# Both first layer norms of a two-block graph kernel from the statistics of x, with x loaded from two queues

## The reference, cut to what matters

```python
def _layernorm(x, axis=-1, eps=1e-05):
    m = jnp.mean(x, axis=axis, keepdims=True)
    v = jnp.var(x, axis=axis, keepdims=True)
    return (x - m) / jnp.sqrt(v + eps)

xn = _layernorm(x, axis=-1)                  # read by the graph branch and by the mix branch
x = x + _L0_gnn_ref(xn, ...) + _L0_mix_ref(xn[None], ...)[0]

# first lines of _L0_mix_ref
xn = _ln(x, g1, be1)                         # a second layer norm, of the first one's output, with scale and bias
kqv = xn @ Wkqv + bkqv
k, q, v = jnp.split(kqv, 3, axis=-1)
```

## Time and profile before

| | us |
|---|---|
| median of three runs | 1988.69 |
| span of the profiled execution, first to last instruction | 1983.8 |
| PE busy in it | 1641.4 |
| DVE busy | 798.2 |
| ACT busy | 506.5 |
| POOL busy | 391.0 |

### The profile page before, as it was taken

How to read it: one execution, slowest core, us unless ns; L and a number is a source line. 1 busy time by engine, 2 the same in 40 slices (tenths; PEclk the granted TensorE clock), 3 DMA queues, 4 the chain that set the end, 5 groups by cost and what they waited for, 6 DMA issues and landing times.

```text
span 1983.8 us, 19802 instructions
## 1 busy us (share of the span) xinstructions
PE 1641.4 (83%) x7770; PEld 1121.7 (57%) x7770; DVE 798.2 (40%) x1511; ACT 506.5 (26%) x734; POOL 391.0 (20%) x248
## 2 busy tenths in 40 slices
PE   1999979989998849888888887899888751999895
PEld 1547645456555638677777763465765641656452
DVE  5021051399502652477777863360334224111100
ACT  1101102012301032477777751100214110101000
POOL 3100021020201120244444423200211002222112
PEclk9999999989998969899999998999998855999997
DMA  4000010100020010101000003000200452699993
GB/s 169 0 0 1 0 44 0 58 1 1 41 86 0 6 64 33 46 14 27 14 13 14 22 8 142 5 22 0 85 0 1 177 224 98 266 406 402 404 418 129
DMA packets 23236, 170.74 MB, mean 86 GB/s; under 512 B 4259, under 2 KB 4805, under 8 KB 16886
## 3 DMA queue, kind: packets, MB, share of 16 engines
q1 hardware_dynamic: 19568, 164.44, 21.0%
q0 software_dynamic: 3584, 5.12, 1.2%
HBM read 153.06 MB, written 16.49 MB: 85 GB/s over the span
## 4 chain that ended last, share of the span: by engine, by line
PE 58%; DMA 15%; DVE 13%; ACT 6%; issue 4%; POOL 2%; another core or an unknown queue 1%; SPq 0%; DVEq 0%; POOLq 0%; ACTq 0%
PE psum L839 15%; DMA out_x<-arena,idx 12%; PE psum L849 9%; PE psum L866 6%; PE psum L980 6%; PE psum L1065 4%; PE psum L858 4%; PE psum L1053 3%; DVE arena_r L1449 3%; PE psum L1035 2%; DMA xf_dram<-arena 2%; DVE neg_max L1428 2%; ACT arena_r L762 1%; DVE ln_st L1219 1%; DVE arena L1227 1%
## 5 line engine op out<-in xcount | busy, mean ns | idle before, releaser
L839 PE MATMUL psum<-arena 125*128 125x512 f32 (+3 forms) x864 | 306.5, 516 | 14.4 <-DMA arena<-in_w_in 11.6
L839 PEld LDWEIGHTS psum<-arena 125*128 125x128 f32 (+1 forms) x864 | 164.1, 190 | 156.2 <-issue 142.2
L866 PE MATMUL psum<-arena 128*125 128x512 f32 (+3 forms) x464 | 162.6, 509 | 17.1 <-DVE arena L1556 9.0
L541 POOL TENSOR_SCALAR arena<-arena,row_inv 125x1250 f32<-125x1250 f32 x40 | 138.4, 3459 | 192.3 <-DVE row_inv L1436 192.3
L1200 PE MATMUL psum<-arena 128*39 128x512 f32 (+1 forms) x704 | 159.1, 609 | 13.2 <-DMA arena<-in_w_down 10.2
L1053 PE MATMUL psum<-ident,arena 125*125 125x125 f32 x800 | 125.6, 283 | 49.8 <-DVE arena_r L1449 48.5
L1449 DVE TENSOR_TENSOR arena_r<-psum,arena_r 125x500 fp32r<-125x500 f32 x200 | 131.9, 672 | 42.1 <-ACT arena_r L762 32.3
L1053 PEld LDWEIGHTS psum<-ident,arena 125*125 125x125 f32 x800 | 102.9, 188 | 63.0 <-DVE arena_r L1449 58.3
L762 ACT ACTIVATE arena_r<-psum 125x500 fp32r<-125x500 f32 x200 | 114.3, 586 | 88.0 <-PE psum L1053 87.8
L866 PEld LDWEIGHTS psum<-arena 128*125 128x125 f32 (+2 forms) x464 | 81.2, 191 | 95.2 <-issue 71.4
L980 PE MATMUL psum<-arena 125*125 125x512 bf16 (+1 forms) x588 | 119.8, 359 | 12.8 <-DVE arena L1340 11.3
(11 more groups left out here) (279 smaller groups left out, 2051.4 us busy)
## 6 DMA issues: line engine op xcount, KB each, us to landing
arena<-in_w_down SPq DMA_DIRECT2D x32, 2816.0 KB, 23.5
arena<-in_w_up SPq DMA_DIRECT2D x32, 682.5 KB, 19.4
a_spill<-arena SPq DMA_DIRECT2D x1, 6103.5 KB
arena<-a_spill SPq DMA_DIRECT2D x1, 6103.5 KB
bc<-k_dram SPq DMA_DIRECT2D x16, 312.5 KB, 4.2
gw<-in_gw SPq DMA_DIRECT2D x2, 2048.0 KB, 10.6
arena<-in_wkqv SPq DMA_DIRECT2D x1, 3072.0 KB, 16.4
arena<-in_x SPq DMA_DIRECT2D x10, 250.0 KB
```

Source lines behind the costliest of these rows:

```text
L541: pool.tensor_scalar(PR[i], PR[i], row_inv[:, i:i + 1], None, ALU.mult).then_inc(p_even, 1)
L839: ins = pe.matmul(o[0:w, lo:hi], lhs(c, m), rhs(c)[:, lo:hi], start=c == 0, stop=c == k - 1)
L866: ins = pe.matmul(o[0:p, 0:w], lhs(c, t), rhs(c, t), start=c == 0, stop=c == k - 1)
```

## The change

The order of the norms is turned round. The statistics are taken once, of x. For a row with variance v, the first norm's output has mean 0 and variance v / (v + e), so the second norm of it is (x - m) / sqrt(v (1 + e) + e * e). GpSimd makes that root for each group, and then the first norm's own root for all ten tiles in one pair of instructions (`xn_rs`, semaphore `xn_rstd`). VectorE writes `XH1` straight from X, a group behind the statistics, and writes `XN` after it. SyncE issues the even tiles of x and `wkqv` right behind them. ScalarE's queue issues the odd tiles and `vec`. GpSimd's bias addition now waits for both norms.

```diff
-LN_ORDER = [(n, g) for n in ("xn", "mix1", "mix2") for g in range(3)]
+LN_ORDER = [(n, g) for n in ("mix1", "mix2") for g in range(3)]
...
-            for t in range(TILES):
+            for t in range(0, TILES, 2):
                 load(f"x{t}", X[:, t], x_v[:, t])
-            load("vec", vec[:], a["vec"])
+            load("wkqv", WKQV, a["wkqv"].rearrange("p (k n) -> p k n", k=C))
             load("edge_rows", edge_rows_i, a["dst_rows"])
             load("edges", edge_i[:, 0:EDGE_TILES], a["src_cols"])
             load("edges", edge_i[:, EDGE_TILES:2 * EDGE_TILES], a["dst_cols"])
-            load("wkqv", WKQV, a["wkqv"].rearrange("p (k n) -> p k n", k=C))
...
-            for g in range(3):
-                rstd("xn", g)
+            for g, (lo, hi) in enumerate(GROUPS):
+                pool.wait_ge(ln_mv, LN_TILES["mix1", g])
+                pool.tensor_scalar(ln_rs[:, lo:hi], ln_mv_t[:, lo:hi, 1], 1.0 + LN_EPS, LN_EPS * LN_EPS,
+                                   ALU.mult, ALU.add).then_inc(ln_eps, 1)
+                pool.wait_ge(ln_eps, LN_NUMBER["mix1", g] + 1)
+                pool.tensor_tensor(ln_rs[:, lo:hi], ln_rs[:, lo:hi], minus_half[:, lo:hi], ALU.pow).then_inc(ln_rstd, 1)
+            done(pool.tensor_scalar(xn_rs[:], ln_mv_t[:, :, 1], LN_EPS, None, ALU.add))
+            pool.tensor_tensor(xn_rs[:], xn_rs[:], minus_half[:], ALU.pow).then_inc(xn_rstd, 1)
...
-            for g in range(3):
-                rstd("mix1", g)
-
             pool.wait_ge(loads["b2"], 16)
-            pool.wait_ge(ln_out, TILES)
+            pool.wait_ge(ln_out, 2 * TILES)
...
+            x_v = a["x"].rearrange("(t p) d -> p t d", p=TOK)
+            for t in range(1, TILES, 2):
+                act.dma_start(X[:, t], x_v[:, t]).then_inc(loads[f"x{t}"], 16)
+            act.dma_start(vec[:], a["vec"]).then_inc(loads["vec"], 16)
             act.wait_ge(loads["vec"], 16)
...
             for g in range(3):
-                stats("xn", g, X, lambda t: dve.wait_ge(loads[f"x{t}"], 16))
-            for g in range(3):
-                normalise("xn", g, X, XN)
-
-            for g in range(3):
-                stats("mix1", g, XN, lambda t: dve.wait_ge(ln_out, LN_OUT["xn"] + t + 1))
-            for g in range(3):
-                normalise("mix1", g, XN, XH1)
+                stats("mix1", g, X, lambda t: dve.wait_ge(loads[f"x{t}"], 16))
+                if g:
+                    normalise("mix1", g - 1, X, XH1)
+            normalise("mix1", 2, X, XH1)
+            dve.wait_ge(xn_rstd, 1)
+            for t in range(TILES):
+                dve.tensor_scalar(XN[:, t], X[:, t], ln_mv_t[:, t, 0:1], xn_rs[:, t:t + 1],
+                                  ALU.subtract, ALU.mult).then_inc(ln_out, 1)
```

More of the change, by code:

```diff
@@ L88 @@
 LN_TILES = {x: sum(GROUPS[g][1] - GROUPS[g][0] for _, g in LN_ORDER[:n + 1]) for n, x in enumerate(LN_ORDER)}
-LN_OUT = {n: TILES * i for i, n in enumerate(("xn", "mix1", "mix2", "ffn", "l1", "moe"))}
+LN_OUT = {n: TILES * i for i, n in enumerate(("mix1", "xn", "mix2", "ffn", "l1", "moe"))}
 def moe_rows():
@@ L128, in build @@
         ln_rs = sb("ln_rs", [TOK, TILES])
+        xn_rs = sb("xn_rs", [TOK, TILES])
         src_f = sb("src_f", [EDGE_TILE, EDGE_TILES])
@@ L285, in build @@
         ln_stats, ln_mv, ln_eps, ln_rstd, ln_out = [sem(n) for n in ("ln_stats", "ln_mv", "ln_eps", "ln_rstd", "ln_out")]
+        xn_rstd = sem("xn_rstd")
         dve_step, pool_step = sem("dve_step"), sem("pool_step")
```

## The result

The changed kernel took 1978.18 us (median of four runs, 1975.41 to 1979.30) against 1988.21 us of the kernel before on the same chip. The ratio is 0.9945, with a 95% interval of 0.993 to 0.996: 10.0 us or half a per cent faster, where 9.4 us were forecast.

What follows compares the result with a forecast made beforehand. Bound by a chain of waits: x's loads until 24.55 us, norms, transposes, copies, k at 51.45. Starting k at 42.1 gains 9.4: 1983.8 - 9.4 + 4.9 = 1979.3 us, range 1971.5 to 1984.7.

Steps and rivals of the forecast that it cites:

- The last wait: Before ScalarE's first copies: `vec` takes turns with `wkqv` rows, lands at 32.4 us; k starts at 42.1.
- 6 us or more after the last tile's statistics: Sign for the forecast: ScalarE's copies, released by `vec`, start at 31 to 34 us, this long after those statistics.
- How many turns: On x's five engines: `vec`'s eight short rows alternate with eight long `wkqv` rows, delaying `vec` until 32.4 us.
- rival B: At the loads: `vec` gets through at 25.1 us; k at 36.2, gain 15.3, time 1973.4; chance 0.26.
- x under `wkqv`: At x's loads: `wkqv` traffic delays x by 1.5 us, out of 0.9 to 4.9; x in at 24.9.
- The 4.9 us: Whole kernel: the runs' median lies 4.9 us above the profiled span of 1983.8, carried over unchanged.
- the span falls by less than k's start does: Whole kernel: a sign that the forecast is wrong, since nothing but a shift was expected after k.
- Two queues: At x's loads: a second queue meets the same five engines and gains nothing; last tile at 23.4 us before `wkqv`'s delay.
- Rival C: At x's loads: the second queue takes other engines; x in at 14.4 us, gain 26, time 1962; chance 0.03.
- D's sign: At x's loads: pairs over 5.7 us apart show two queues costing rate; at half rate, time 2003; chance 0.04.
- The norms: On VectorE and GpSimd before k: by the norms alone k could start at 34.8 us, x in at 24.9.
- Rival E: After k: three more half-clock TensorE stretches, 1.7 us each, take back 5.1 of 9.4; time 1984.4; chance 0.09.

Runs made afterwards that it cites:

- control: The changed kernel plus asserted bounds on the third number loaded for each block of the adjacency count; 1978.1 us, ratio 0.9949 to the kernel before.
- vec_first: The control with `vec` issued ahead of the odd tiles on ScalarE's queue; 1985.9 us, ratio 0.9990 to the kernel before.
- wkqv_held: The control with `wkqv` issued only once the last two tiles of x have landed; 1974.6 us, ratio 0.9921 to the kernel before.
- rows120_only: The kernel before, bounds added, each x tile loaded as 120 and 5 rows on its one queue; 1977.0 us, ratio 0.9952.
- norms_only: The control's new norms with the loads of the kernel before (one queue: x, `vec`, edges, `wkqv`); 1975.4 us, ratio 0.9929.
- rows120_norms: The control's new norms, one queue issuing `vec`, x tiles as 120 and 5 rows, then `wkqv`; 1964.2 us, ratio 0.9888.

## Why the prediction was right, and where three of its terms were not

**The last wait.** The forecast said that `vec` would take x's place, because its short rows take turns with the 24 KB rows of `wkqv`; first copy at 32.4, k at 42.1. It was 31.63 and 41.48. The mechanism is shown by three runs that change only the turns, and by the packets. A long row takes 24.6 KB / (421 / 16) = 0.93 us, a 6 KB row 0.23. Behind the last tiles `vec` landed 3.75 us in the control (31.07 less 27.32), 1.04 with short rows: four turns of the one or of the other, three for rows and one for the four-byte write that reports an engine's share as complete. In halves it was 7.9 us, all eight turns. With `wkqv` held it was 0.1. And the earlier trace rows had the sign of it. Of the signs set down for the forecast, though, "6 us or more after the last tile's statistics" failed (3.6), and so did a table load long before (it ended 1.65 us before the copy) and last statistics at 24 to 27 (28.0).

**How many turns.** I took eight, 7.5 us; there were four. Five of `vec`'s eight rows on each engine passed by 26.9 in the control's packets, beside the even queue's last rows of x. That is rival B's condition ("the odd queue runs slightly ahead") met halfway. `vec_first` shows the same phase on its other side, where it cost 7 us against the control. The Trainium skill ("DMA: Bandwidth & Descriptors", "Queues, rings and completion order") has an engine drain typically 9 to 17 rows of one queue at a turn; the packets do not agree with that for these loads: in the control and in `vec_first` a turn was one row.

**x under `wkqv`.** The delay of x by `wkqv`'s traffic was 4.6 us, and I took 1.5 out of 0.9 to 4.9. The upper end, the 0.98 us of before's last tile and not the 0.17 of the one ahead of it, was the measure: two pairs were 2.0 and 2.2 us late, 1.05 for a tile. The reason given for leaving that end aside, the end of a burst, did not hold. And the early start of `wkqv` bought nothing, since `wkqv` itself landed at 35.3 (32.0 after its issue at 3.29), later than before's 34.6. I had it on the eleven engines at 5 us; its issue was only through at 10.5, 7.2 us after it began, most likely held by the rows of x queued ahead of it, since with none ahead it took 0.36 us (`wkqv_held`). This term and the number of turns are 3.1 and 3.8 us off and opposite in sign. The forecast of k's start, 0.6 off, owes that to luck.

**The 4.9 us.** The time forecast, 1979.3, hides a second pair of this kind. The span after was forecast at 1974.4 and measured 1977.3, 2.9 more; what lies around it was 1.8 and not 4.9, 3.1 less. By the medians the gain was 10.0, by the two profiled executions 6.5 while k's start moved by 10.0, so the sign "the span falls by less than k's start does" was met in this pair. In the working, the forecast's own range adds up to 1977.0 to 1984.4 from its terms, not 1976 to 1983.5, E's upper figure to 1987.8, not 1986, and B's first copy to 26.3, not 26.5; none of the three changes the outcome.

**Two queues.** As forecast they gave nothing: five engines, by `wkqv_held`'s 130 GB/s at a share of 0.34. That the row count sets the engines is shown by `rows120_only`: 120 rows and 5 in place of 125 gave a share of 0.96 for 0.33. The Trainium skill ("DMA: Bandwidth & Descriptors", "Why a DMA increments its semaphore by 16 and not by 1") has the number of engines follow from the rows by division, and the trace agrees. Rival C is out. D's sign, pairs more than 5.7 us apart, did appear (6.2 and 6.0), but its cause is out too: with two queues and no `wkqv` the pairs were 4.0 apart.

**The norms.** Forecast: by the norms alone k could start at 34.8 with x in at 24.9. `norms_only` started it at 35.28 with x in at 25.2, released by `wkqv`; its copies were done at 35.1, so the norms' own limit was at 35.1 or earlier and is not seen closer than that. The XN normalise, the edge work and the bias additions stayed covered: VectorE still stood 67.7 us before L1269, where the earlier trace rows had 76.7.

**After k.** Rival E was partly there in the profiled executions. One half-clock stretch that before fell on the start of k was absent, which made the lead 11.5 us at the XN turn; then later ones gave part of it back. Two stretches of the changed kernel, over short matmuls and the first eight long ones behind them:

```profile
209.60:213.00 3.40, 3.40 (x11) 2.37 (x11) 0.16 (x1) 0.00 (x0) 0.00 (x0) 0.50 0.00 0
213.00:216.40 3.40, 3.40 (x6) 1.33 (x5) 0.00 (x0) 0.00 (x0) 0.00 (x0) 0.50 0.00 0
```

and of the kernel before, from the start of the same eight:

```profile
221.80:225.20 3.40, 3.40 (x6) 1.53 (x6) 0.16 (x1) 0.00 (x0) 0.00 (x0) 0.50 0.00 0
225.20:228.60 3.40, 3.40 (x9) 1.52 (x8) 0.00 (x0) 0.00 (x0) 0.00 (x0) 1.00 0.00 0
```

Before, 1.2 GHz (0.50) lasts 3.4 us there and then gives way to 2.4; after, it lasts 6.8, at full work, and from the XN turn to the end of those eight matmuls the lead falls from 11.5 to 9.8 us. By the attention's transposes 7.3 us of 11.5 are left (first start 823.1 for 830.4), and 6.5 in the span. After and before:

```profile
L1061 PE MATMUL psum<-ident,arena x800: 268/273/373, 823.1 to 1174.0; 125*125 125x125 f32 x160
L1053 PE MATMUL psum<-ident,arena x800: 267/273/373, 830.4 to 1180.1; 125*125 125x125 f32 x160
```

Such stretches fall differently in each kernel, and runs of one kernel scatter by 2 to 12 us. Over nine experiments the medians moved by 0.3 to 1.1 times what k's start did, six of them by 0.9 or more. So k's start is the sharper instrument here, and no difference of 2 or 3 us in the medians is taken as shown.

## What to carry to other kernels

Ask first how many DMA engines a load runs on: a share of 0.33 at 128 GB/s said five of 16, and then a second queue brought nothing, while splitting 125 rows into 120 and 5 brought 10 us. A small load that something waits for is badly placed in one queue while another moves long rows on the same engines: here it landed 3.75 us behind the tiles ahead of it. Put it where it lands first, and watch what it does to the loads behind it: `vec_first` lost by it, and `rows120_norms`, with one queue, did not. Of a change in two halves test each: here the norms won 16 us at k's start and the loads gave 6 of them back.

## What was not expected of the hardware

With five engines on x's 2 KB rows and eleven on `wkqv`, all 16 busy, the sum was 278 GB/s; with all 16 on `wkqv` it was 421. Both sides slowed down, though no engine carried both kinds of row: in the control's packets a 2 KB row took 0.13 us instead of 0.08, a 24 KB row about 1.35 instead of 0.92. So the limit is one that the engines share. x alone on nearly all engines (a share of 0.96, in `rows120_only`) was no better: 247 GB/s. Shorter rows of `wkqv` did not change it (288 GB/s from 12 to 20). Why x's rows pull the sum down, whether by their 2 KB length, by their place in memory or by the 125-row tiles, these runs do not tell, and it stays open. It cost the changed kernel 4.6 us, and the best version still pays for it.

A queue that issues a small 128-row load ahead of x also started x late: in `vec_first` the odd queue's first row of x ran at 5.2, the even queue's at 1.7. The first tile of the even queue landed alone at 5.6 where pairs came at 7.5, and that lead, about a tile, lasted until `wkqv` began.
